# Destination one-hots of two edge tiles at a time, formed by one two-operand comparison with broadcast operands, in a graph transformer on one Trainium2 core

## What is computed

```python
e = jax.nn.leaky_relu(a1[src] + a2[dst], negative_slope=NEG_SLOPE)
m = jax.ops.segment_max(e, dst, num_segments=n)
w = jnp.exp(e - m[dst])
denom = jax.ops.segment_sum(w, dst, num_segments=n)
alpha = w / jnp.maximum(denom[dst], 1e-16)
msg = alpha[:, :, None] * ft[src]
agg = jax.ops.segment_sum(msg, dst, num_segments=n)
res = jnp.einsum('nhd,od->nho', hv, W_res)
out = jax.nn.relu((agg + res).reshape(n, H * DOUT))
```

## Time and profile before

| what | value |
|---|---|
| median of 3 runs | 2149.12 us (2142.5 to 2151.97) |
| the profiled execution's own time | 2141.64 us |
| its span, first to last instruction | 2139.8 us |
| PE busy | 1928.0 us (90%) |
| PE weight loads busy | 1234.0 us (58%) |
| DVE busy | 757.1 us (35%) |
| ACT busy | 397.3 us (19%) |
| mean granted TensorE clock | 0.949 |

### The profile page before, as it was taken

The page is one execution under the profiler, slowest core; times in us unless marked ns, Lnnn a source line. Parts: engine busy times, 40 slices in busy tenths (PEclk is TensorE's granted clock), DMA queues, the critical chain, the costliest instruction groups (busy, mean ns, idle before and its releaser), DMA issues.

```text
span 2139.8 us, 23079 instructions
## 1 busy us (share of the span) xinstructions
PE 1928.0 (90%) x7603; PEld 1234.0 (58%) x7604; DVE 757.1 (35%) x1715; ACT 397.3 (19%) x1046; POOL 132.0 (6%) x223
## 2 busy tenths in 40 slices
PE   5999999998999999779995999999999999399990
PEld 3555566566433446646663875555578589266560
DVE  3211322676688879411112511141111133311113
ACT  2331210024211112100100332000221211111110
POOL 0000000000000000011112300000000000111114
PEclk9999999999999999579997999999999999599995
DMA  6004000000000101424554410110010012434537
GB/s 174 0 1 155 2 0 1 19 1 0 20 29 28 42 21 44 162 74 176 188 180 131 139 59 0 44 45 0 0 45 1 0 59 61 159 125 170 183 118 223
DMA packets 58416, 154.05 MB, mean 72 GB/s; under 512 B 12574, under 2 KB 23218, under 8 KB 57893
## 3 DMA queue, kind: packets, MB, share of 16 engines
q1 hardware_dynamic: 34053, 87.05, 11.6%
q0 software_dynamic: 13200, 36.25, 5.5%
q10 hardware_dynamic: 11088, 29.77, 3.8%
HBM read 121.76 MB, written 34.78 MB: 73 GB/s over the span
## 4 chain that ended last, share of the span: by engine, by line
PE 86%; DMA 5%; DVE 4%; issue 2%; ACT 1%; DVEq 1%; POOL 1%; POOLq 0%; ACTq 0%; SPq 0%
PE PS L605 22%; PE PS L821 11%; PE PS L906 10%; PE PS L615 7%; PE PS L753 5%; PE PS L996 4%; PE PS L932 4%; PE PS L1016 4%; PE PS L669 4%; PE PS L973 3%; PE PS L959 3%; DMA WS<-in_fW 2%; DMA YG<-expert_rows,IDXA 2%; PE PS L884 1%; PE PS L803 1%
## 5 line engine op out<-in xcount | busy, mean ns | idle before, releaser
L605 PE MATMUL PS<-WS,XT 128*125 128x384 f32 x960 | 312.5, 487 | 1.4 <-issue 1.4
L821 PE MATMUL PS<-WR,F 125*65 125x500 f32 (+1 forms) x720 | 262.2, 518 | 2.5 <-DVE WR L1572 2.5
L605 PEld LDWEIGHTS PS<-WS,XT 128*125 128x125 f32 x960 | 180.0, 188 | 129.0 <-issue 2.6
L1572 DVE SCALAR_TENSOR_TENSOR WR<-RB,U,AT 125x500 f32<-125x500 f32 (+1 forms) x360 | 212.5, 647 | 22.0 <-PE PS L821 13.7
L906 PE MATMUL PS<-WS,XGT 128*128 x624 | 208.0, 490 | 0.0
L821 PEld LDWEIGHTS PS<-WR,F 125*65 125x65 f32 x720 | 97.6, 139 | 142.8 <-issue 99.8
L906 PEld LDWEIGHTS PS<-WS,XGT 128*128 128x128 f32 x624 | 117.7, 192 | 77.3 <-issue 2.5
L615 PE MATMUL PS<-XT,WS 128*128 128x416 f32 (+1 forms) x432 | 151.2, 512 | 0.0
L1698 DVE TENSOR_TENSOR YS<-PS,EBB 128x768 f32<-128x768 f32 x50 | 47.9, 958 | 270.5 <-PE PS L906 209.6
L615 PEld LDWEIGHTS PS<-XT,WS 128*128 128x128 f32 x432 | 81.6, 189 | 69.2 <-issue 69.2
L753 PE MATMUL PS<-OHS,OHD 125*125 125x418 bf16 x564 | 110.8, 351 | 0.0
(11 more groups left out here) (263 smaller groups left out, 1968.8 us busy)
## 6 DMA issues: line engine op xcount, KB each, us to landing
expert_rows<-YS ACTq DMA_DIRECT2D x50, 384.0 KB
WS<-in_ewT SPq DMA_DIRECT2D x8, 2304.0 KB, 10.6
WS<-in_fW SPq DMA_DIRECT2D x16, 1152.0 KB, 7.8
WS<-in_w SPq DMA_DIRECT2D x5, 2304.0 KB, 9.8
xn_rows<-XN ACTq DMA_DIRECT2D x20, 336.0 KB
RB<-expert_rows SPq DMA_DIRECT2D x12, 488.3 KB
WS<-in_wp SPq DMA_DIRECT2D x2, 2304.0 KB, 11.8
WS<-in_W SPq DMA_DIRECT2D x2, 2304.0 KB, 8.3
```

The lines of the kernel that those rows point to most:

```text
L605: last = nc.tensor.matmul(ps[0:T, 0:HC], lhsT[:, k, t * T:(t + 1) * T], w[:, k, b * HC:(b + 1) * HC], start=(k == 0), stop=(k == KC - 1))
L821: last = nc.tensor.matmul(PS[0:DW, 2 * (u % 2) + j, 0:n], F[:, s, 2 * p + j, :], WR[:, k % WSLOTS, j, 0:n], start=(s == 0), stop=(s == NT ...
L1572: V.scalar_tensor_tensor(out=WR[:, k % WSLOTS, j, 0:nt * T], in0=RBS[u % RSLOTS][:, j, 0:nt * T], scalar=U[:, s, h:h + 1], in1=AT[:, s, t0 ...
```

## The change

The destination numbers of all tiles are also kept as float16, in a new tile `EDH` (125 x 160), copied from PSUM by one more DVE instruction ahead of the copy into `ES`. In the loop, the two `OHD` comparisons of slots `k` and `k+1` (even `k`), each a comparison of a float16 row with one number per partition, become one comparison of two streams of 250 elements: the 125 column numbers of the block read twice, and the two tiles' numbers, each read 125 times. Before it stands one wait, for the later of the two slots to be free. Two signals for two `OHD` become one, so a turn now counts six on `oh_ready` where it counted eight.

```diff
+    EDH = sb("EDH", [T, ET], F16)
...
-                    pe.wait_ge(oh_ready, u * (2 * SLOTS) + 2 * k + 2)
+                    pe.wait_ge(oh_ready, u * (SLOTS + SLOTS // 2) + k + k // 2 + 2)
...
         ps = full(0)
+        V.tensor_copy(EDH, ps[0:T, ET:2 * ET])
         V.tensor_copy(ES.rearrange("p a b -> p (a b)"), ps[0:T, 0:320]).then_inc(dve_emptied, 1)
...
                 for k in range(SLOTS):
-                    dve.wait_ge(oh_free, u * SLOTS + k + 1)
-                    V.tensor_scalar(OHD[:, k, :], iota[0:T, g * T:(g + 1) * T], ES[:, 1, bass.ds(tile + k, 1)],
-                                    None, ALU.is_equal).then_inc(oh_ready, 1)
+                    if k % 2 == 0:
+                        dve.wait_ge(oh_free, u * SLOTS + k + 2)
+                        V.tensor_tensor(OHD[:, k:k + 2, :], iota[0:T, g * T:(g + 1) * T].unsqueeze(1).to_broadcast([T, 2, T]),
+                                        EDH[:, bass.ds(tile + k, 2)].unsqueeze(2).to_broadcast([T, 2, T]),
+                                        ALU.is_equal).then_inc(oh_ready, 1)
                     V.tensor_scalar(OHS[:, k, :], iota[0:T, :], ES[:, 0, bass.ds(tile + k, 1)],
                                     None, ALU.is_equal).then_inc(oh_ready, 1)
```

## The result

The changed kernel took 2151.82 us (median of 20 runs, 2146.45 to 2239.59), the kernel before 2145.61 us (20 runs, 2137.16 to 2152.18). The ratio is 1.0026, with a 95% interval of 1.0015 to 1.0038: 5.6 us slower, between 3.2 and 8.2. I had forecast 7.7 us slower. The highest of the 20 runs was disturbed and is left out of the ratio.

The account below looks back on a forecast made before the run. Each count block was taken to start at TensorE's pace, 0.522 us a slot, and end at DVE's, 0.618. Terms 0.2 + 5.2 + 0.7 + 1.35 + 0.24 = +7.7 us on the median 2149.12 gave 2156.8 us, range 2146 to 2165.

Parts of the forecast that it names:

- The sign: Whole kernel: slower, by 0.36%; chance 0.24 of slower by over 0.5%, 0.03 of faster by over 0.5%.
- the later wait: Each block's refill on DVE starts one TensorE slot later, 0.522 us in each of ten blocks: +5.2 us.
- The comparison's price: DVE's two-stream OHD comparison takes 0.333 us start to start against 0.330 for two single ones: +0.2 us over 74 pairs.
- Two OHS close together: A pair's OHS come 0.453 us apart, under TensorE's 0.522, so each block's last slot begins 0.069 us late: +0.7 us.
- the extra wait of 0.050 us at every second pair: In steady pace DVE waits for a pair's second slot, seen free at 1.742 against 1.692 us, 27 times: +1.35 us.
- the one on what can be told: Whole kernel: measurement can tell about 0.5%, 10.7 us, from no change; chance 0.73 of a result within 0.5%.
- The copy at the start: DVE's extra copy of 160 numbers lies on the chain to the first normalised rows: +0.24 us, nothing if a load hides it.
- A: DVE's comparison takes two elements per cycle, 0.203 us, partly lost to waits: +1.7 us, 2150.8 us; chance 0.12.
- B: Fast comparison on DVE and freed slots seen sooner than 1.07 us, so the wait costs nothing: 2139.9 us, 0.43% faster; chance 0.03.
- C: DVE's comparison keeps 0.130 us of fixed time and costs 0.390 us: +10.6 us, 2159.7 us; chance 0.22.

Follow-up runs that it names:

- wait_only: Kernel before, comparisons still single, but DVE waits for a pair's later slot at even slots and not at odd ones; ratio to before 1.0040.
- doubled: Changed kernel with each destination number stored twice, OHD rows widened from 125 to 126 and the EDH copy moved to just ahead of the count; ratio to before 1.0002.
- singles_together: Kernel before in the changed kernel's order: wait for the pair's later slot, two single OHD comparisons, then two OHS; ratio to before 1.0041.
- source_first: Changed kernel with the two-stream comparison and the later slot's wait moved between the pair's two OHS, the first needing only its own slot; ratio to before 1.0015.
- wait_four: Kernel before with one wait per turn, for all four slots to be free; ratio to before 1.0248.
- before_again: Kernel before, unchanged, run once more for its profile; blocks of 12 at full clock took 6.55 us.

## Why the prediction was right or wrong

**The sign, and the reason, held.** I had forecast 0.36% slower and the runs gave 0.26%, inside the range. The main term was the later wait, 10 x 0.522 = 5.2 us. In wait_only it measures 0.54 us a block, 5.4 us. DVE's resumption at 1.58 us in the changed kernel, where I had 1.59, shows the same. From first to last slot the last block grew by 0.53 us (6.15 to 6.68).

**The comparison's price held.** I took 0.333 us from rows of two-stream instructions with 4-byte inputs. In the timeline above OHS starts 0.34 us behind the block's first comparison and 0.32 us behind the next. At 1.24 us a pair nothing was gained, as I had it. That this was the lower of two rates is now measured: 418 against 288 ns. The Trainium skill, Vector Engine (DVE) Microarchitecture Reference, section 5.1, reports the lower rate for one element read again and again as second source. The two runs agree with it, though they don't set the step apart from the odd rows. The Trainium skill's page VectorE: DVE Perf Modes gives, in its perf-mode tier table, a two-stream op on 16-bit SBUF data twice the rate: so it is in doubled, and not in the changed kernel.

**Two OHS close together** was costed at 0.069 us a block. The size held, the place didn't. The difference between singles_together and wait_only is 0.08 us, and it lies inside the last slot. I had its loads begin 0.069 us late; they begin as soon as its OHS is there, 0.45 us behind the first slot's:

```profile
568.04 0.45 PEld L754 LDWEIGHTS PS<-OHS,OHD 125*125 125x125 bf16 x3
```

This is the last slot of the last block, in the timeline from 568 us on; its pair began at 567.59 and stands above as one row of six. But from its first load to the load behind it pass 0.49 us (568.04 to 568.53), where a slot that stands alone took 0.40 (556.06 to 556.46 in the kernel before): the pair's first slot still holds TensorE's matmuls. The last slot's first matmul starts 0.13 us behind its load, where it started together with it before. source_first has the same: in its blocks of 16 the last slot begins at 8.63 us (8.62 before), and all of the 0.1 us left comes behind that.

**The step that failed is the extra wait of 0.050 us at every second pair, 1.35 us in all. The changed kernel has none of it.** I had said that DVE, starting a pair, finds the second slot of the pair before the last not yet free, at 1.742 us against 1.692. The changed kernel's steady pairs come at 1.24 us without such a wait, in the long block too, which grew by 0.70 and not by 1.21 us. The trace of doubled shows which figure was wrong, because there the comparison is short enough for the wait to come up (the row of three loads is from the timeline of PEld from 555.80 us on, which parts them from the pair's first three):

```profile
554.79 0.99 DVE L1532 TENSOR_SCALAR OHS<-iota,ES 125x1250 bf16<-125x1250 f16 x2
...
555.70 0.29 DVE L1528 TENSOR_TENSOR OHD<-iota,EDH 125x252 bf16<-125x252 f16 x1
...
555.84 0.45 PEld L754 LDWEIGHTS PS<-OHS,OHD 125*125 125x125 bf16 x3
...
556.92 0.29 DVE L1528 TENSOR_TENSOR OHD<-iota,EDH 125x252 bf16<-125x252 f16 x1
...
558.04 0.28 DVE L1528 TENSOR_TENSOR OHD<-iota,EDH 125x252 bf16<-125x252 f16 x1
```

DVE's pairs come 1.12 us apart where nothing holds them (556.92 to 558.04) and 1.22 where the wait does (555.70 to 556.92), at every second pair, as the mechanism had it. The pair's second OHS started at 555.24 (two that end at 555.78, 0.54 us each), its slot's loads at 555.84, and DVE went on at 556.92. So the way back was 1.08 us, the 1.07 that I had. But the slot began 0.60 us behind its OHS's start, where I had 0.672, for I had put the second slot a full 0.522 us behind the first. In sum DVE sees it free at 1.68 us and not at 1.742. In the changed kernel DVE isn't ready before 1.692, so the wait never shows.

**A second step failed, the one on what can be told.** I had put the smallest difference that this kernel's measurement can tell from none at about 0.5%, 10.7 us, from three runs, and gave 0.73 to a difference within it. With 20 runs of each kernel the interval is 0.12% to either side, and the 0.26% stands clear of none.

**The copy at the start** is there: the timeline has it start at 9.61 us and ES's at 9.85, the 0.24 us I had.

```profile
9.61 0.33 DVE L1329 CAST EDH<-PS 125x160 f16<-125x160 f32 x1 [1.28 <-PE PS L625]
9.85 0.48 DVE L1330 COPY ES<-PS 125x320 f32<-125x320 f32 x1
```

The first transposes for the projections began at 25.67 us, 25.63 before, with the edge list 0.11 us earlier in this execution (9.61 against 9.72). So about 0.15 of the 0.24 us reached them, as far as two executions can say.

With 6.3 us for the blocks and 0.15 to 0.24 us for the copy the sum would have been 6.5 us, 0.30%, well inside the measured interval. The rivals: A's rate didn't occur, and when doubled made it occur the result was A's (0.0%, I had +1.7 us). A's own sum had waits of 0.180 us, where doubled shows 0.10. B asked for a cheap way back, and the idle time of 1 us a turn in wait_four speaks against it. C's price of 0.390 us wasn't there.

**The whole stretch would have misled me without the block lengths.** Between the profiles of the two kernels, the time from the first count load to the first product behind the count grew by 11.3 us, not by 6.3. The rest is clock: the changed kernel's profile has three more block starts at half clock, at 1.66 us each, 5.0 us (below).

## What to carry to other kernels

Merging the work of two buffers into one instruction also merges their waits. Before doing so, find how long it takes from a consumer's start on a buffer until the producer goes on with it (here 1.07 us, of which 0.52 are the consumer's own loads) and how far the producer is ahead. Here the consumer caught up within each block, so a wait for one buffer more was paid in full once a block, and a merged instruction that took as long as the two before it won nothing back. Put work that needs only the first buffer ahead of the merged instruction. And busy time saved on an engine (7.8 us here) says nothing of the kernel's time while its waits grow as much. Last, this two-stream comparison, with a broadcast that stands still in the innermost dimension and odd rows, ran at half of the rate that it had with each number stored twice and even rows.

## What the runs showed of the hardware

TensorE's granted clock fell from 2.4 to 1.2 GHz around the starts of some blocks, in every profile, for a few microseconds. Ahead of it TensorE had stood for 1.15 and about 1.0 us, waiting for ScalarE's copies and for its own table reads, after a whole block of work. The same gaps stand ahead of blocks that started at full clock. In four neighbouring windows (486 to 501, 501 to 515, 515 to 528 and 528 to 542 us) the mean granted clock, 1.00 for 2.4 GHz, was 0.97, 0.91, 1.00 and 1.00 in the first profile of the kernel before, where one fall lay across the first two, and 0.89, 1.00, 0.87 and 0.88 in before_again.

The loads show the price. In the changed kernel this is a block start at full clock and one at half:

```profile
559.98 1.46 PEld L728 LDWEIGHTS PS<-WBD,XT 128*125 128x125 f32 x12
...
545.90 2.81 PEld L728 LDWEIGHTS PS<-WBD,XT 128*125 128x125 f32 x12
```

Each fall costs about 1.66 us: the time from clearing the banks to the first count load rises from 1.78 to up to 3.4 us, or the first slots take the rest. One execution of the kernel before had one fall in the last nine block starts, another six, and the stretch differed by 8.5 us between them without any edit. This is more than the change is worth. Over the whole span the time of a run goes with its mean granted clock: of 35 runs of the kernel before, measured beside the experiments, the fastest took 2135.65 us at 0.953 and the slowest 2158.03 us at 0.943. The mean over these 35 is 0.949, and over the changed kernel's 19 undisturbed runs it is 0.949 too, so unequal clocks are an unlikely source of the 5.6 us; the clocks of the 20 runs that they were compared with aren't on record. What decides which block start falls wasn't settled.
